# Fourth stage of a four-stage attention and expert kernel: every product as three rounded ones

## The reference, cut to what matters

```
x = x + jnp.tanh(g_xattn[0]) * _L0_xattn_ref(_layernorm(x), ...)
x = x + jnp.tanh(g_ffn[0]) * _L0_ffn_ref(_layernorm(x), ...)        # 32 experts, 6 per token
x = x + jnp.tanh(g_xattn[1]) * _L1_xattn_ref(_layernorm(x), ctx, ctx)
x = x + jnp.tanh(g_ffn[1]) * _L1_ffn_ref(_layernorm(x), ...)        # 8 experts, 2 per token
...
# in _L1_ffn_ref: H = 512, I = 352, E = 8
def expert_step(acc, ws):
    gw, uw, dw, ce = ws
    out = jax.nn.silu(x @ gw) * (x @ uw) @ dw
    return (acc + ce[:, None] * out, None)
```

## Time and profile before

| | |
|---|---|
| median of 3 runs | 1208.76 us (1204.76 to 1212.23) |
| the profiled execution | 1218.6 us, its span 1216.7 us |
| granted TensorE clock, mean over the span | 0.934 of full |
| stage 4, first turn of a tile to the last scaling | 881 to 1206 us of the span |

### The profile page before, as it was taken

One profiled execution on the slowest core, in us unless ns is written; L12 is line 12 of the kernel. 1 busy time (PEld: TensorE's weight loads), 2 busy tenths in 40 slices (PEclk: granted clock), 3 DMA queues, 4 the chain that ended last, 5 costly groups with the idle time before them and its releaser, 6 DMA issues.

```text
span 1216.7 us, 13055 instructions
## 1 busy us (share of the span) xinstructions
PE 1056.7 (87%) x4351; PEld 705.6 (58%) x4351; DVE 479.6 (39%) x1148; ACT 341.5 (28%) x537; POOL 386.3 (32%) x340
## 2 busy tenths in 40 slices
PE   5886698979979989995599899999089999999996
PEld 4333243469869778884385657675055655565553
DVE  5678757333424544332854644515011111111110
ACT  3464141023323433332243332311012222221221
POOL 0004767525435445453002020202013332333232
PEclk9788699989989999997699999999589999999999
DMA  9111011179989998965406120209913323332330
GB/s 330 70 52 43 11 62 36 51 275 277 260 274 263 263 242 234 246 159 84 159 18 57 47 44 9 52 18 307 320 48 64 62 54 62 68 63 54 64 70 8
DMA packets 52800, 148.52 MB, mean 122 GB/s; under 512 B 12243, under 2 KB 12627, under 8 KB 47296
## 3 DMA queue, kind: packets, MB, share of 16 engines
q1 hardware_dynamic: 24752, 81.09, 21.0%
q0 software_dynamic: 24160, 44.03, 18.8%
q10 hardware_dynamic: 3824, 22.57, 5.8%
HBM read 109.76 MB, written 41.08 MB: 124 GB/s over the span
## 4 chain that ended last, share of the span: by engine, by line
PE 63%; DMA 16%; DVE 10%; issue 4%; ACT 3%; POOL 3%; ACTq 0%; SPq 0%; POOLq 0%; DVEq 0%
PE pb L561 15%; PE pb L577 8%; DMA acc_rows<-big 7%; PE pb L449 7%; PE pb L534 5%; DMA big<-hn_rows,big 5%; PE pb L308 4%; PE pb L310 4%; PE pb L309 4%; DVE big L874 4%; PE pb L315 3%; PE pb L403 3%; PE pb L371 3%; POOL acc_rows L1284 2%; DMA list_rows<-big 2%
## 5 line engine op out<-in xcount | busy, mean ns | idle before, releaser
L561 PE MATMUL pb<-big 128*128 x624 | 193.2, 463 | 4.1 <-issue 4.1
L449 PE MATMUL pb<-big 128*128 128x192 f32 x1024 | 174.1, 329 | 2.1 <-ACT bigr L721 1.3
L449 PEld LDWEIGHTS pb<-big 128*128 128x128 f32 x1024 | 169.8, 192 | 6.4 <-issue 3.4
L561 PEld LDWEIGHTS pb<-big 128*128 128x128 f32 x624 | 116.6, 192 | 63.4 <-issue 6.2
L1253 POOL DMA_INDIRECT list_rows<-big x96 | 95.8, 998 | 137.2 <-DVE big L886 108.5
L1284 POOL DMA_INDIRECT acc_rows<-big x64 | 95.4, 1491 | 138.2 <-DMA acc_rows<-big 53.5
L308 PE MATMUL pb<-bigr 128*128 128x512 f32 (+2 forms) x320 | 132.9, 415 | 7.0 <-DVE big L882 4.6
L1311 POOL DMA_INDIRECT out<-big x39 | 61.8, 1584 | 207.4 <-ACT big L854 207.4
L310 PE MATMUL pb<-bigr 128*128 128x512 f32 (+2 forms) x320 | 127.6, 399 | 0.0
L309 PE MATMUL pb<-bigr 128*128 128x512 f32 (+2 forms) x320 | 127.1, 397 | 0.0
L874 DVE TENSOR_TENSOR big<-big,pb 128x352 f32<-128x352 f32 (+4 forms) x87 | 33.4, 383 | 206.5 <-ACT big L848 192.4
(11 more groups left out here) (119 smaller groups left out, 1167.8 us busy)
## 6 DMA issues: line engine op xcount, KB each, us to landing
big<-in_we SPq DMA_DIRECT2D x32, 1024.0 KB, 8.0
rawr<-in_we SPq DMA_DIRECT2D x32, 512.0 KB, 4.4
big<-in_we ACTq DMA_DIRECT2D x1, 8704.0 KB, 41.5
hn_rows<-big SPq DMA_DIRECT2D x32, 256.0 KB, 2.0
big<-in_we ACTq DMA_DIRECT2D x1, 6528.0 KB, 54.4
big<-in_x SPq DMA_DIRECT2D x4, 1024.0 KB, 15.3
acc_rows<-big SPq DMA_DIRECT2D x16, 256.0 KB, 4.2
big<-acc_rows SPq DMA_DIRECT2D x16, 256.0 KB, 4.8
```

Of the source, the lines that this page charges most:

```text
L449: r = e.matmul(ps[:, m * CAP:(m + 1) * CAP], WR[b % 4][:, at_:at_ + 128], XT[b % 2][:, k, :], start=(k == 0), stop=(k == 3))
L561: r = e.matmul(ps[:, 0:I1], XT1[b % 2][:, k, :], W1[:, bass.ds(r0 + (q * 4 + k) * I1, I1)], start=(k == 0), stop=(k == 3))
```

## The change

Only stage 4 is changed, apart from places of buffers. All its products go through `three`, so that gate and up are 24 float32r matmuls with 352 columns in place of 8 float32 ones, and down is 9 with 512 columns in place of 3. For that, each tile's weights are split into high and low parts after the tile's expert is known:

- ScalarE gets `wgh`, `wuh` and `wdh`: copies of the gate (128 x 1408), up (128 x 1408) and down (128 x 1536) weights of the tile's expert into float32r. VectorE gets `wgl`, `wul` and `wdl`: the subtractions for the low parts, `wdl` for two of the three blocks of the down weights (128 x 1024). GpSimd gets `wdl` for the third block (128 x 512). There is one buffer for each high and each low part (WGH, WGL, WUH, WUL, WDH1, WDL1).
- The register with the expert's place is now read by ScalarE (ahead of `wgh`), by VectorE (ahead of `wgl`) and by GpSimd (ahead of `wdl`), not by TensorE.
- The turned tokens and the turned intermediate get a high part (ScalarE `turnt`, `flipt`) and a low part (VectorE `turnt`, `flipt`). The two VectorE copies of `flipt` go.
- `upt` is split into `gatet` and `upt`. Gathers run three tiles ahead, with semaphores of their own (`l_g4`). The intermediate is padded with zeros to 384 columns (`zero4`, two fills before the first tile). `yt` 1 and 2 wait for the stores of stage 3 (`l_o`). Some small buffers of stage 3 move into constants that are no longer needed.

```diff
-        pe4 = "turnt.0 " + words(lambda n: f"upt.{n} " + (f"turnt.{n + 1} " if n + 1 < NT else "") + (f"downt.{n - 1} " if n else "") + f"flipt.{n}", NT) + f" downt.{NT - 1}"
-        act4 = "turnt.0 " + words(lambda n: f"silut.{n} " + (f"turnt.{n + 1} " if n + 1 < NT else "") + (f"yt.{n - 1}" if n else ""), NT) + f" yt.{NT - 1}"
-        dve4 = words(lambda n: f"mult.{n} flipt.{n}", NT)
-        pool4 = words(lambda n: (f"fetcht.{n + 2} " if n + 2 < NT else "") + (f"addt.{n - 1}" if n else ""), NT) + f" addt.{NT - 1}"
+        pe4 = "turnt.0 " + words(lambda n: f"gatet.{n} upt.{n} " + (f"turnt.{n + 1} " if n + 1 < NT else "") + (f"downt.{n - 1} " if n else "") + f"flipt.{n}", NT) + f" downt.{NT - 1}"
+        act4 = "turnt.0 wgh.0 wuh.0 " + words(lambda n: f"silut.{n} " + (f"wgh.{n + 1} turnt.{n + 1} wuh.{n + 1} " if n + 1 < NT else "")
+                                              + (f"yt.{n - 1} " if n else "") + f"wdh.{n} flipt.{n}", NT) + f" yt.{NT - 1}"
+        dve4 = "zero4 turnt.0 wgl.0 wul.0 " + words(lambda n: f"mult.{n} " + (f"wgl.{n + 1} turnt.{n + 1} wul.{n + 1} " if n + 1 < NT else "")
+                                                    + f"wdl.{n} flipt.{n}", NT)
+        pool4 = words(lambda n: (f"fetcht.{n + 3} " if n + 3 < NT else "") + (f"addt.{n - 1} " if n else "") + f"wdl.{n}", NT) + f" addt.{NT - 1}"
...
@@ TensorE
-                    r0 = regs[b] = e.value_load(ETK[0:1, b:b + 1], min_val=0, max_val=7 * WE1)
-                    for q, ps in ((0, pg), (1, pu)):
-                        for k in range(4):
-                            r = e.matmul(ps[:, 0:I1], XT1[b % 2][:, k, :], W1[:, bass.ds(r0 + (q * 4 + k) * I1, I1)], start=(k == 0), stop=(k == 3))
+                elif kind in ("gatet", "upt"):
+                    q = 0 if kind == "gatet" else 1
+                    wh, wl = ((WGH, WGL), (WUH, WUL))[q]
+                    e.wait_ge(s_dve, dv("turnt", b))
+                    e.wait_ge(s_dve, dv("wgl" if q == 0 else "wul", b))
...
+                    three(e, PB[2 + 2 * (b % 2) + q][:, 0:I1], [(XH1[b % 2][:, k, :], XL1[b % 2][:, k, :], wh[:, k * I1:(k + 1) * I1], wl[:, k * I1:(k + 1) * I1])
+                                                               for k in range(4)]).then_inc(s_pe, c.up())
...
+                    e.wait_ge(s_dve, dv("wdl", b))
+                    e.wait_ge(s_pool, b + 1)
+                    three(e, PB[6 + b % 2][:, :], [(NTH[b % 2][:, k * 128:(k + 1) * 128], NTL1[b % 2][:, k * 128:(k + 1) * 128], WDH1[:, k * D:(k + 1) * D], WDL1[:, k * D:(k + 1) * D])
+                                                   for k in range(3)]).then_inc(s_pe, c.up())
...
@@ ScalarE
+                elif kind in ("wgh", "wuh", "wdh"):
+                    at_, n, dst, user = dict(wgh=(0, 4 * I1, WGH, "gatet"), wuh=(4 * I1, 4 * I1, WUH, "upt"), wdh=(8 * I1, 3 * D, WDH1, "downt"))[kind]
...
+                        e.wait_ge(s_pe, pe(user, b - 1))
+                    if kind == "wgh":
+                        regs[b] = e.value_load(ETK[0:1, b:b + 1], min_val=0, max_val=7 * WE1)
+                    prev()
+                    e.activation(dst, w1[:, bass.ds(regs[b] + at_, n)], ACT.Copy).then_inc(s_act, c.up())
...
@@ VectorE
+                elif kind in ("wgl", "wul", "wdl"):
...
+                    e.wait_ge(s_act, av(kind[0:2] + "h", b))
+                    if b:
+                        e.wait_ge(s_pe, pe(user, b - 1))
+                    if kind == "wgl":
+                        regs[b] = e.value_load(ETK[0:1, b:b + 1], min_val=0, max_val=7 * WE1)
...
+                    tensor(lo, w1[:, bass.ds(regs[b] + at_, n)], hi.bitcast(F32), ALU.subtract)
...
@@ GpSimd
+                elif kind == "wdl":
+                    e.wait_ge(s_act, av("wdh", b))
+                    if b:
+                        e.wait_ge(s_pe, pe("downt", b - 1))
+                    r0 = e.value_load(ETK[0:1, b:b + 1], min_val=0, max_val=7 * WE1)
+                    e.tensor_tensor(WDL1[:, 2 * D:3 * D], w1[:, bass.ds(r0 + 8 * I1 + 2 * D, D)], WDH1[:, 2 * D:3 * D].bitcast(F32), ALU.subtract).then_inc(s_pool, 1)
```

More of the change, by code:

```diff
@@ L118, in program @@
         rawr = second_name("rawr", 17152, 34816, F32)
+        later = second_name("later", 38144, 53120, F32R)
+        slots = second_name("slots", 40192, 50176, F32R)
+        with nc.sbuf_tensor("w1", [128, 34816], F32) as w1:
+            pass
         big = ctx.enter_context(nc.sbuf_tensor("big", [128, 53120], F32))
@@ L133, in R, with LR, SLOT @@
             return S(off - 13056, *shape, mem=bigr)
+        def LR(off, *shape):
+            return S(off - 38144, *shape, mem=later)
+        def SLOT(off, *shape):
+            return S(off - 40192, *shape, mem=slots)
         def RAW(off, *shape):
@@ L227, in program @@
         SWD = late(6, D)
+        inter = late(6, D)
+        AC1 = [late(D) for _ in range(2)]
         SS1 = [late(D) for _ in range(2)]
-        AC1 = [late(D) for _ in range(2)]
         SB1, CC1 = late(12), late(4, 5 * E1)
@@ L239, in program @@
             c1.append(c)
[L240 to L241 removed]
+        old = taker(CON_AT + C_TR, CON_AT + C_TR + T * K0)
+        recs = [(old(4, K1, 2), old(4, K1).bitcast(I32)) for _ in range(4)]
+        old = taker(CON_AT + C_INV, CON_AT + C_INV + 128)
+        ca = {"ST": old(4, 6), "MV": old(4, 2), "RS": old(4), "R2": old(4)}
         NB, NC, NTL = late(8), late(8), late(8)
         NI = late(8).bitcast(I32)
[L244 to L252, removed]
+        CMP, ETF, BLF = late(NT, 8), late(NT), late(NT)
+        ETK, BLI = old(NT).bitcast(I32), old(1).bitcast(I32)
+        assert late.at[0] <= RING + 9216 + 8 * I1
+        WGH, WGL = SLOT(RING + 9216, 4 * I1), SLOT(RING + 9216 + 4 * I1, 4 * I1)
+        WUH, WUL = SLOT(RING + 2048, 4 * I1), SLOT(RING + 2048 + 4 * I1, 4 * I1)
+        WDH1, WDL1 = SLOT(RING + 5120, 3 * D), SLOT(RING + 5120 + 3 * D, 3 * D)
+        NTH, NTL1 = ([LR(RING + 768 * i + 384 * q, 384) for i in range(2)] for q in range(2))
+        four = taker(RING + 9216 + 8 * I1, 53120)
+        XH1, XL1 = ([LR(four.at[0] + 1024 * i + 512 * q, 4, 128) for i in range(2)] for q in range(2))
+        four.at[0] += 2048
+        IN1 = [four(384), four(384)]
+        SL1 = [S(CON_AT + C_CM, I1), S(RING + 1536, I1)]
+        G1 = [S(CON_AT + NCONST + 512 * i, 512) for i in range(3)]
+        YS1 = [S(CON_AT + NCONST + 1536, 512), *AC1]
         mask_m = CON[:, C_CM:C_CM + 64].unsqueeze(1).broadcast_to([128, 8, 64])
@@ L268, in program @@
         l_g = [sem(f"l_gather{i}") for i in range(4)]
+        l_g4 = [sem(f"l_gathert{i}") for i in range(3)]
         l_rd = [sem(f"l_down{i}") for i in range(3)]
@@ L859, in _ @@
             c = Counter()
+            regs = {}
             def prev():
@@ L1227, in _ @@
                     both(AC1[j % 2], PB[j][:, :], TG[:, 3:4], xr[b][:, j, :], ALU.mult, ALU.add)
+                elif kind == "zero4":
+                    e.wait_ge(s_pe, pe_end3)
+                    for i in range(2):
+                        prev()
+                        e.memset(IN1[i][:, I1:384], 0.0).then_inc(s_dve, c.up())
+                elif kind == "turnt":
+                    e.wait_ge(s_act, av("turnt", b))
+                    if b >= 2:
+                        e.wait_ge(s_pe, pe("upt", b - 2))
+                    tensor(XL1[b % 2].rearrange("p a b -> p (a b)"), PB[0][:, :], XH1[b % 2].rearrange("p a b -> p (a b)").bitcast(F32), ALU.subtract)
+                elif kind in ("wgl", "wul", "wdl"):
+                    at_, n, hi, lo, user = dict(wgl=(0, 4 * I1, WGH, WGL, "gatet"), wul=(4 * I1, 4 * I1, WUH, WUL, "upt"), wdl=(8 * I1, 3 * D, WDH1, WDL1, "downt"))[kind]
+                    e.wait_ge(s_act, av(kind[0:2] + "h", b))
[3 more added lines that the diff above has]
+                        regs[b] = e.value_load(ETK[0:1, b:b + 1], min_val=0, max_val=7 * WE1)
+                    if kind == "wdl":
+                        n, lo, hi = 2 * D, lo[:, 0:2 * D], hi[:, 0:2 * D]
+                    tensor(lo, w1[:, bass.ds(regs[b] + at_, n)], hi.bitcast(F32), ALU.subtract)
                 elif kind == "mult":
```

69 lines of the change are left out of this document (37 added, 32 removed).

## The result

The changed kernel takes 1321.82 us (median of 4 runs, 1302.07 to 1328.92), the kernel before 1210.49 beside it: ratio 1.084, 95% interval 1.066 to 1.103. Forecast were 1311 us and 102 us more.

A forecast was written before the change was run, and what follows sets the result against it. TensorE was taken to bound stage 4 at 8.08 us per tile; after the change a serial chain of 9.75 plus 0.85 for the clock gives 10.6. 38 beats add 96 us, the ends 3 and 3: 1311 us, range 1262 to 1365.

The forecast's parts named there:

- The chain: Stage 4, from the end of one tile's upt to the next's, through ScalarE, VectorE, TensorE: 9.75 us at full clock.
- The matmul of 352 columns: Stage 4 gate and up on TensorE: 0.160 us per float32r matmul, bounds 0.147 and 0.227; 24 take 3.84 us.
- The register reads: Stage 4, ahead of wgh on ScalarE and wgl on VectorE: read and address 0.8 us each, ScalarE's delaying wgh by 0.3.
- The clock: Stage 4, TensorE idling 2.9 us per tile lets its clock fall: 0.85 us per tile, bounds 0 and 1.7.
- The ends: First split before stage 4's first gate and up, and last down product after the last upt: about 3 us more each.
- GpSimd's block at nothing: Stage 4, third block of the down weights' low part, subtracted on GpSimd: costed at nothing, hidden behind the chain.
- the limit of 2 to 3: Stage 4, GpSimd's subtraction would decide only if it took over 2 to 3 us, making downt late.
- The estimate of 1.1 us: GpSimd's subtraction in stage 4, about 2.6 cycles per element by the Trainium skill: 1.1 us, not used in the sum.
- an expected 56 us of saving on TensorE: Stage 4, TensorE's work falls from 8.08 to 6.65 us per tile: 56 us gained over 39 tiles if it stayed the bound.

The follow-up runs named there:

- silu_first: The changed kernel with silut waiting for the end of gatet alone and mult for upt in its place: 1218.4 us, timed again 1221.74, ratio 1.018.

## Why the prediction was right

**The chain.** Forecast link by link from silu's start: `wgh` at 0.9, `wgl` done at 4.75, tokens at 5.57, silu again at 9.75. Measured in the shortest beats: `wgh` at 0.64, `wgl` done at 4.4, tokens at 5.3, silu at 9.43. That this order costs the most is shown by silu_first, which breaks it and gets 85.5 of 98.7 us back, the clock's and the held reads' part among them.

**The matmul of 352 columns.** 0.160 taken between 0.147 and 0.227; the chain has 0.16.

**The register reads.** 0.8 us each was right for VectorE, from the end of `wgh` to the start of `wgl` (0.77), of which the read costs 0.64. For ScalarE it was wrong in both directions: beside silu the read costs nothing, but held by the add it costs 0.56 in about half of the tiles. On average that makes 0.3, what was forecast, by another mechanism than forecast; that the two sizes agree is luck.

**The clock.** 0.85 per beat was taken, the middle of 0 and 1.7. Measured: 10.45 less 9.43 for the chain less 0.3 for held reads leaves 0.7. The stretch at 1.2 GHz costs 11 x 0.13 = 1.4 us in the tile shown, some tiles have none, as supposed, and the two beats of 12.8, where the clock stayed low for 6.8 us, have twice that. Filling the idle time gave back only 14.3 / 38 = 0.4 of it; more reads were held then. The trace is of the quickest of the four executions, which also had the highest granted clock (0.916, the others 0.902 to 0.908), so the clock may have cost more in the others; there is no trace of these.

**The ends.** 3.5 and 4.0 us for 3 and 3. In the chain of the changed kernel's end, GpSimd's block, which was costed at nothing, stands in the way of the last down product, and most of that product's matmuls come in steps of 0.43, where they take 0.23 at the full clock:

```profile
1281.78 1.19 POOL out L1383
...
1283.39 1.76 POOL slots L1375
...
1285.29 0.47 PE pb L331
```

**GpSimd's block at nothing.** Right for the beat of this kernel, for the reason given: it hides behind the chain. Its listed 1.87 us lie under the limit of 2 to 3 from which it would decide. The estimate of 1.1 us from the Trainium skill (GPSIMD Engine Reference, Performance versus the Vector engine) is somewhat under the 1.27 of the first tile and the 1.32 behind the add's issue. The price that the prediction left out, because no run showed it, is real and larger than the 1.1 us there: 2.4 us of VectorE's time in a tile where GpSimd goes first (3.65 for 1.23). In the changed kernel VectorE went first in 34 of 36 tiles. Not every subtraction reads two operands from the on-chip memory, as the prediction has it: those for the tokens and the intermediate (`later`) read one of theirs from `pb`, where the matmuls write.

So forecast and result agree within 4 us of stage 4. The mechanism was the forecast one: one chain through single buffers with silu at its head. That the agreement is so close is in part luck: a chain 0.3 shorter than forecast, held reads of 0.3 that weren't in it, and a clock that cost 0.15 less, taken as the middle of two bounds.

## What to carry to other kernels

When work is moved off a full engine, write down who makes the operand, into which buffer, and which instruction must have ended before that buffer is free: a single buffer and one wait too late turned an expected 56 us of saving on TensorE into 99 us of loss; the kernel that gains has a second slot, an earlier wait for silu, earlier register reads, another order and one product fewer split. Give split products only to those matmuls for which the helpers have time: in these runs the kernels with two of three were faster than those with all three, though they differ in their order too. A register that a dynamic address needs is read ahead of the wait that its user sits behind, not after it, and a helper block on GpSimd goes where VectorE is not subtracting, or has time to spare.

## What the hardware showed unexpectedly

- A register read from on-chip memory by ScalarE takes 0.28 us, but 0.76 to 0.85 in 48 of the 53 cases (two kernels) where it began 0.83 to 0.93 us after the issue of an indirect add had ended; it then ends about 1.69 us after that issue.
- A VectorE subtraction of 1024 columns takes 1.23 us when it goes ahead of one of 512 columns on GpSimd, and mostly 3.65 when it comes behind it. GpSimd's takes 1.27 to 1.33 us of its own; it is listed with 1.87 where it overlaps the add's issue ahead of it, and with 2.3 where it overlaps VectorE's.
- Issuing an indirect add takes 1.54 to 1.64 us, unless VectorE is in a subtraction of two operands in on-chip memory when the issue begins; then the issue ends 1.42 to 1.52 us after that subtraction (up to 3.0 us in all), also in kernels without any GpSimd arithmetic.
